# A decoder layer on one core: the bf16 identity copied earlier, and in the last FFN both outer convolution taps on VectorE through PSUM, rounding by ScalarE, three y buffers

## The chip, the cores and the metric

The kernel runs on one core of a Trainium2 chip. The metric is the device time of one execution in microseconds. Engines are named as in the profile: PE (TensorE), PEld (its weight loads), DVE (VectorE), ACT (ScalarE), POOL (GpSimd), SP (SyncE, here only a DMA queue).

## What is computed

The input is 4 sequences of 1024 tokens of width 512, in fp32. Three residual blocks follow each other, each on a layer norm of its input: self-attention with 16 heads and ALiBi bias; a local attention-free block with its own FFN ("cross FFN", 512 to 2048 to 512 with ReLU and layer norms); and a quantised FFN with a convolution in the middle ("last FFN"):

```python
h = bit_linear(x, w1)                     # x to 8-bit integers per token, w1 to -1, 0, 1
h = depthwise_conv1d(h.transpose(0, 2, 1), conv_w, conv_b)   # 3 taps along the tokens, and a bias
h = jax.nn.silu(h.transpose(0, 2, 1))
return bit_linear(h, w2)                  # h to 8-bit integers per token: scale = 127 / max|h| of the token
```

Rounding to integers is done by adding and then taking away 1.5 x 2^23 in fp32.

## The kernel before, in words

The stages run one after the other on all engines: projections, attention, `mix_in`, `mix_out`, `cross_ffn`, `quantised_ffn`. The last three share one program block: each engine has one instruction stream, written out by hand, and meets the others only through semaphores. Nothing is reordered; an instruction that waits holds all that stands behind it on its engine.

**The seam between `mix_out` and `cross_ffn`.** On POOL, `mix_out`'s `gpsimd` calls `load_vectors` (L1983, four DMA issues), then `scale_and_shift` for the last rows (two passes over each of six tiles of 128x512, and a store of each half), and then `cross_ffn`'s `gpsimd` begins, whose first instruction (L1992) copies the identity to bf16 as `ident16`. On PE, `cross_ffn`'s `tensor` begins with two waits, for `mix_out`'s last read of the PSUM banks that its own tiles lie on, and for the identity:

```python
pe.wait_ge(*before["emb"])        # DVE's last residual add, L1787
pe.wait_ge(ident16_ready, 1)
```

`ident16` itself is first used much later, to turn the quantised rows (L2056). The weights come in four chunks: SP loads (L1945, L1948), ACT rounds to the high part (L2083), DVE takes the difference (L2139).

**The last FFN.** The hidden layer is worked as 8 units (half a sequence, 512 tokens) of 16 blocks (128 hidden channels on the partitions, 512 tokens along the free axis). One slot `s` of the outer loop starts block `s`; later steps of a block stand a fixed number of slots behind (SILU_AT and so on), and every engine's stream is the same loop over slots. A block's way:

- PE multiplies it into `acc` (L2448), two banks.
- DVE multiplies by the tokens' units into `y` (`dequantise`, L2568), a row of 514 with one edge value on either side, two buffers.
- ACT copies one edge value (`set_edge`, L2523), and makes `centre` = tap 1 times y plus bias, in PSUM (L2530), and `right_tap` = tap 2 times y shifted, in SBUF (L2534).
- DVE adds tap 0 times y to `centre`, giving `conv` in SBUF (`add_left`, L2577); POOL adds `right_tap` to it (`add_right`, L2406).
- ACT applies SiLU (L2514); PE turns the block (L2457); DVE takes the maximum over its channels (`find_max`, L2585).

When 16 maxima of a unit are there, DVE works out the scales (`scales`, L2591 to L2602, five small operations and a diagonal matrix), PE spreads them over the partitions (L2465), ACT copies them out as `scale_row` (L2548). Then POOL multiplies each block by it (`scale_block`, L2412), and DVE rounds to bf16 (`round_block`, L2610), and PE makes the second product (L2475, and L2501 for the last unit). DVE adds the residual (`finish`, L2618), once in four slots. Each second unit PE also makes the products of the columns at the halves' edge (L2429), 128 small ones.

DVE's slot before is: maximum, y, left tap, rounding, and in some slots scales and `finish`. ACT's is: edge, centre, right tap, SiLU.

## Time and profile before

| | |
|---|---|
| three runs | 3474.91, 3478.45, 3482.97 us, median 3478.45 |
| profiled execution | 3476.95 us, span 3475.4 us, mean granted clock 0.967 |
| busy in the span | PE 3150.0 (91%), PEld 2284.4 (66%), DVE 2338.6 (67%), ACT 1766.6 (51%), POOL 1176.7 (34%) |
| stages by the first instruction of each | cross FFN from 2280.1 us, last FFN's slots from 3040.1 us |

The shares are an average over stages with different limits; each stage is read by itself. The profile's chain of the work that ended last covers only the last FFN here. The instructions are issued in pipeline: a timeline's next start on the same engine can lie before the listed end of the one in front.

### The profile page before, as it was taken

The numbers are of one execution on the slowest core, as the hardware profiler recorded it, in microseconds if no ns is written. First come the engines' busy times: TensorE is split into PE (matmuls) and PEld (weight loads), VectorE is DVE, ScalarE is ACT, GpSimd is POOL, SyncE is SP. The second block draws the span as 40 slices with busy tenths as digits, with TensorE's granted clock in tenths as the row PEclk, the third lists the DMA queues.
The fourth block names the chain that finished last, engine by engine and source line by source line (L and its number), as shares of the span: only waits on it lengthen the run. The fifth ranks groups of instructions, "written<-read, shape, count | busy, mean of one in ns | idle before, by whom it ended". The sixth has DMA issues, their size and how long they took to land. (4 is left out here: it accounts for less than half of the span.)

```text
span 3475.4 us, 57137 instructions
## 1 busy us (share of the span) xinstructions
PE 3150.0 (91%) x19234; PEld 2284.4 (66%) x19234; DVE 2338.6 (67%) x4193; ACT 1766.6 (51%) x3130; POOL 1176.7 (34%) x909
## 2 busy tenths in 40 slices
PE   6999899999999999979998788879999999768886
PEld 5777566666666666657776677668888888534443
DVE  5562788888888888745644588835555444589996
ACT  3331788888888888712222322232222222176662
POOL 3343411231123112244442355521111111068886
PEclk9999899999999999989999899989999999899999
DMA  6774321222122212265552644431111110300112
GB/s 215 248 238 165 98 64 58 76 77 63 58 75 76 62 57 76 76 213 210 197 202 111 183 130 123 142 111 41 41 43 42 41 43 31 110 25 31 62 49 67
DMA packets 239351, 350.53 MB, mean 101 GB/s; under 512 B 31792, under 2 KB 129104, under 8 KB 239184
## 3 DMA queue, kind: packets, MB, share of 16 engines
q1 hardware_dynamic: 208256, 290.41, 25.9%
q0 software_dynamic: 8912, 32.82, 2.9%
q10 hardware_dynamic: 22016, 25.17, 2.0%
q8 instruction: 93, 1.52, 0.2%
q14 instruction: 74, 0.61, 0.1%
HBM read 210.68 MB, written 137.64 MB: 100 GB/s over the span
## 5 line engine op out<-in xcount | busy, mean ns | idle before, releaser
L887 DVE CUSTOM_DVE_ANT_0 attend_scores<-attend_scores,attend_bias_table 128x1024 f32<-128x1024 f32 x512 | 630.4, 1231 | 164.5 <-PE attend_scores L741 161.2
L814 ACT ACTIVATE attend_probs<-attend_scores,attend_neg_max 128x1024 f32<-128x1024 f32 x512 | 571.3, 1116 | 141.1 <-DVE attend_neg_max L887 131.0
L753 PE MATMUL attend_turned<-ident,attend_probs 128*128 128x128 f32 x4096 | 557.4, 275 | 12.6 <-DVE attend_probsT L895 12.5
L753 PEld LDWEIGHTS attend_turned<-ident,attend_probs 128*128 128x128 f32 x4096 | 473.2, 141 | 120.9 <-DVE attend_probsT L895 29.8
L741 PE MATMUL attend_scores<-attend_k_stack,attend_q_stack 96*128 96x512 f32 x1024 | 373.7, 447 | 17.8 <-DMA attend_q_stack<-qk_parts 14.7
L822 ACT COPY attend_probsT<-attend_turned 128x512 f32<-128x512 f32 x640 | 359.1, 583 | 24.7 <-PE attend_turned L753 23.1
L2235 DVE TENSOR_TENSOR cross_ffn_h_lo<-cross_ffn_hidden,cross_ffn_h_hi 128x512 fp32r<-128x512 f32 x128 | 96.0, 755 | 363.9 <-ACT cross_ffn_h_hi L2126 363.2
L703 POOL TENSOR_TENSOR attend_out_parts<-attend_out_full,attend_out_parts 128x256 fp32r<-128x256 f32 x64 | 46.5, 726 | 847.1 <-ACT attend_out_parts L829 847.1
L768 PE MATMUL attend_out_acc<-attend_probsT,attend_v_in 128*32 128x256 f32 x4096 | 312.9, 390 | 0.7 <-DVE attend_out_full L905 0.7
L741 PEld LDWEIGHTS attend_scores<-attend_k_stack,attend_q_stack 96*128 96x128 f32 x1024 | 154.4, 190 | 174.7 <-issue 157.3
L895 DVE COPY attend_probsT<-attend_turned 128x512 f32<-128x512 f32 x384 | 263.5, 686 | 1.3 <-PE attend_turned L753 1.3
L2123 ACT ACTIVATE cross_ffn_hidden<-cross_ffn_h_acc,cross_ffn_b_cols 128x512 f32<-128x512 f32 x128 | 88.2, 689 | 282.3 <-PE cross_ffn_h_acc L2030 263.3
L2028 PE MATMUL cross_ffn_h_acc<-cross_ffn_aT_hi,cross_ffn_w_hi 128*128 128x512 f32 x512 | 200.4, 391 | 23.4 <-POOL cross_ffn_ident L1992 22.7
L697 POOL TENSOR_TENSOR attend_bias_table<-attend_neg_distance,attend_slope_now 128x1920 f32<-128x1920 f32 x64 | 214.8, 3387 | 1.4 <-POOL attend_slope_now L689 0.2
L2406 POOL TENSOR_TENSOR quantised_ffn_conv<-quantised_ffn_conv,quantised_ffn_right_tap 128x512 f32<-128x512 f32 x128 | 177.9, 1390 | 96.6 <-DVE quantised_ffn_conv L2577 96.5
L2041 PE MATMUL cross_ffn_out_acc<-cross_ffn_w_hi,cross_ffn_h_hi 128*128 128x512 f32 x512 | 204.2, 399 | 4.4 <-DVE cross_ffn_h_lo L2235 4.4
L2126 ACT CAST cross_ffn_h_hi<-cross_ffn_hidden 128x512 fp32r<-128x512 f32 x128 | 79.6, 622 | 239.2 <-PE cross_ffn_out_acc L2043 238.2
L2029 PE MATMUL cross_ffn_h_acc<-cross_ffn_aT_hi,cross_ffn_w_lo 128*128 128x512 f32 x512 | 200.2, 391 | 0.0
L2030 PE MATMUL cross_ffn_h_acc<-cross_ffn_aT_lo,cross_ffn_w_hi 128*128 128x512 f32 x512 | 200.0, 391 | 0.0
L2042 PE MATMUL cross_ffn_out_acc<-cross_ffn_w_lo,cross_ffn_h_hi 128*128 128x512 f32 x512 | 200.0, 391 | 0.0
L2043 PE MATMUL cross_ffn_out_acc<-cross_ffn_w_hi,cross_ffn_h_lo 128*128 128x512 f32 x512 | 199.8, 390 | 0.0
L2412 POOL TENSOR_TENSOR quantised_ffn_h_scaled<-quantised_ffn_h,quantised_ffn_scale_row 128x512 f32<-128x512 f32 x128 | 162.9, 1275 | 12.6 <-ACT quantised_ffn_scale_row L2548 7.9
(291 smaller groups left out, 6650.0 us busy)
## 6 DMA issues: line engine op xcount, KB each, us to landing
qk_parts<-qkv_qk_out SPq DMA_DIRECT2D x64, 512.0 KB, 3.2
attend_k_stack<-qk_parts SPq DMA_DIRECT2D x192, 128.0 KB, 2.5
attend_q_stack<-qk_parts SPq DMA_DIRECT2D x192, 128.0 KB, 2.7
qkv_wq_raw<-L_ffn_w POOLq DMA_DIRECT2D x16, 1024.0 KB, 7.6
o_parts<-attend_out_parts ACTq DMA_DIRECT2D x64, 256.0 KB, 2.5
carried_o_in<-o_parts SPq DMA_DIRECT2D x32, 512.0 KB, 6.2
qkv_x_in<-x SPq DMA_DIRECT2D x8, 1024.0 KB, 5.9
v_rows<-qkv_v_out SPq DMA_DIRECT2D x32, 256.0 KB, 3.4
```

Source lines behind the costliest of these rows:

```text
L697: pool.tensor_tensor(bias_table[:, h], neg_distance[:, :], slope_now[:, h:h + 1].to_broadcast([P, SPAN]), ALU.mult).then_inc(table_ready, 1)
L741: last = pe.matmul(scores[:, i % 2, k * HALF:(k + 1) * HALF], q_stack[:, h, queries], k_stack[:, h, k * HALF:(k + 1) * HALF], start=True, ...
L753: last = pe.transpose(turned[:, x, c], probs[:, i % 2, k * P:(k + 1) * P], ident[:, :])
L768: last = pe.matmul(out_acc[rows, 0:QG], v_in[:, c, rows], probsT[:, (qg - 1) % 2, c, h], start=(c == 0), stop=(c == TB - 1))
L814: act.activation(probs[:, i % 2], scores[:, i % 2], ACT.Exp, bias=neg_max[:, i % 4:i % 4 + 1], scale=-1.0, accum_out=den[:, qg % 2, j, h:h ...
L822: act.copy(probsT[:, qg % 2, x * HB:(x + 1) * HB, h, j * P:(j + 1) * P], turned[:, x]).then_inc(copied[x], 1)
L887: dve.tensor_tensor_reduce(scores[:, i % 2], scores[:, i % 2], bias_table[:, h, at:at + T], -1.0, BIG, ALU.add, ALU.min, neg_max[:, i % 4: ...
L895: dve.tensor_copy(probsT[:, qg % 2, HB:TB, h, j * P:(j + 1) * P], turned[:, 1]).then_inc(copied[1], 1)
L2028: pe.matmul(out, w1_hi[:, c, cols], aT_hi[:, c], start=c == 0, stop=False)
L2029: pe.matmul(out, w1_lo[:, c, cols], aT_hi[:, c], start=False, stop=False)
L2030: last = pe.matmul(out, w1_hi[:, c, cols], aT_lo[:, c], start=False, stop=c == KB - 1)
L2041: pe.matmul(out_acc[:, t], hi, w2_hi[:, j], start=j == 0, stop=False)
```

## The change

`load_vectors` now ends with the bf16 copy of the identity, and `gpsimd` of the cross FFN no longer begins with it. In the last FFN, `add_left` writes its sum back to `centre` in PSUM, and a new `add_right` on DVE adds the third tap from y into `conv`; POOL's `add_right` and ACT's right tap are gone. Rounding of the first seven units goes to ACT as two passes (`round_up` in place, `round_down` to bf16), with the SiLU between them; the last unit's stays on DVE (`round_last`) with a semaphore of its own. y has three buffers; the taps are added two slots behind y instead of one, and SiLU, turn, maximum, spread, scaling and rounding come one slot earlier. The waits that guard y and `centre` now name `right_added`; constants' waits count 9 memsets instead of 5.

```diff
@@ cross_ffn: load_vectors, gpsimd
                 pool.dma_start(tile[:, :], row(vector, 0, D)).then_inc(rows_loaded, 16)
+            pool.tensor_copy(ident16[:, :], ident[:, :]).then_inc(ident16_ready, 1)
 
         def gpsimd(pool):
-            pool.tensor_copy(ident16[:, :], ident[:, :]).then_inc(ident16_ready, 1)
@@ quantised_ffn: constants and tiles
+    YR = 3
-    SILU_AT, TURN_AT, MAX_AT = 3, 4, 5
-    SPREAD_AT, SCALE_AT, ROUND_AT = HB + 5, HB + 6, HB + 7
+    TAPS_AT, SILU_AT, TURN_AT, MAX_AT = 2, 2, 3, 4
+    SPREAD_AT, SCALE_AT, ROUND_AT = HB + 4, HB + 5, HB + 6
-        y = sb("y", [P, 2, 2, HALF + 2])
+        y = sb("y", [P, 2, YR, HALF + 2])
-        right_tap = sb("right_tap", [P, 2, HALF])
+        round_up_col = sb("round_up_col", [P, 1])
+        round_down_col = sb("round_down_col", [P, 1])
@@ gpsimd
+            pool.memset(round_up_col[:, :], ROUND).then_inc(const_step, 1)
+            pool.memset(round_down_col[:, :], -ROUND).then_inc(const_step, 1)
-            for s in range(2):
+            for s in range(YR):
                 pool.memset(y[:, 0, s, 0:1], 0.0).then_inc(const_step, 1)
                 pool.memset(y[:, 1, s, HALF + 1:], 0.0).then_inc(const_step, 1)
-            def add_right(i):
-                pool.wait_ge(right_ready, i + 1)
-                pool.wait_ge(left_added, i + 1)
-                pool.tensor_tensor(conv[:, i % CR], conv[:, i % CR], right_tap[:, i % 2], ALU.add).then_inc(right_added, 1)
             def scale_block(i):
                 u, f = divmod(i, HB)
                 pool.wait_ge(scale_row_ready, u + 1)
-                past(pool, hq_ready, i - 1)
+                if u == LAST and f >= 2:
+                    pool.wait_ge(last_hq_ready, f - 1)
+                else:
+                    past(pool, hq_ready, i - 1)
@@ scalar
+            def round_up(i):
+                act.wait_ge(h_scaled_ready, i + 1)
+                act.activation(h_scaled[:, i % 2], h_scaled[:, i % 2], ACT.Identity, bias=round_up_col[:, :]).then_inc(h_raised, 1)
+
+            def round_down(i):
+                u, f = divmod(i, HB)
+                act.wait_ge(h_raised, i + 1)
+                if f == 0:
+                    past(act, out_ready, (u - 1) * HT)
+                act.activation(hqT[:, u % 2, f], h_scaled[:, i % 2], ACT.Identity, bias=round_down_col[:, :]).then_inc(hq_ready, 1)
@@ scalar: taps_of
-                past(act, left_added, i - 1)
+                past(act, right_added, i - 1)
...
-                past(act, right_added, i - 1)
-                act.wait_ge(y_edged, i + 1)
-                act.activation(right_tap[:, i % 2], y[:, s, i % 2, 2:HALF + 2], ACT.Identity, scale=taps[:, f, 2:3])\
-                    .then_inc(right_ready, 1)
@@ scalar: loop over slots
                     taps_of(s)
+                r = block_at(s, ROUND_AT)
+                if r is not None and r < LAST * HB:
+                    round_up(r)
                 i = block_at(s, SILU_AT)
                 if i is not None:
                     silu(i)
+                if r is not None and r < LAST * HB:
+                    round_down(r)
@@ vector
             def add_left(i):
...
+                dve.scalar_tensor_tensor(out=centre[:, i % 2], in0=y[:, u % 2, i % YR, 0:HALF], scalar=taps[:, f, 0:1], in1=centre[:, i % 2],
+                                         op0=ALU.mult, op1=ALU.add).then_inc(left_added, 1)
+
+            def add_right(i):
+                u, f = divmod(i, HB)
+                dve.wait_ge(left_added, i + 1)
                 past(dve, silu_done, i - CR + 1)
-                dve.scalar_tensor_tensor(out=conv[:, i % CR], in0=y[:, u % 2, i % 2, 0:HALF], scalar=taps[:, f, 0:1], in1=centre[:, i % 2],
-                                         op0=ALU.mult, op1=ALU.add).then_inc(left_added, 1)
+                dve.scalar_tensor_tensor(out=conv[:, i % CR], in0=y[:, u % 2, i % YR, 2:HALF + 2], scalar=taps[:, f, 2:3], in1=centre[:, i % 2],
+                                         op0=ALU.mult, op1=ALU.add).then_inc(right_added, 1)
...
-            def round_block(i):
+            def round_last(f):
+                i = LAST * HB + f
                 dve.wait_ge(h_scaled_ready, i + 1)
...
+                dve.tensor_scalar(hqT[:, LAST % 2, f], h_scaled[:, i % 2], ROUND, -ROUND, ALU.add, ALU.add).then_inc(last_hq_ready, 1)
@@ vector: loop over slots
+                c = block_at(s, TAPS_AT)
+                if c is not None:
+                    add_left(c)
                 i = block_at(s, MAX_AT)
                 if i is not None:
                     find_max(i)
+                if c is not None:
+                    add_right(c)
                 if s < SLOTS:
                     dequantise(s)
-                i = block_at(s, 1)
-                if i is not None:
-                    add_left(i)
                 i = block_at(s, ROUND_AT)
-                if i is not None:
-                    round_block(i)
+                if i is not None and i >= LAST * HB:
+                    round_last(i - LAST * HB)
```


## Rows read from the trace of the kernel before

**Rows 1.** Busy time by stretch: stretch, length, each engine, clock, DMA share, GB/s.
```profile
2400.00:2900.00 500.00, 495.44 (x2281) 405.09 (x2280) 242.53 (x585) 136.62 (x219) 59.14 (x44) 1.00 0.13 40
3110.00:3300.00 190.00, 154.17 (x968) 79.92 (x967) 177.04 (x287) 128.01 (x253) 163.22 (x125) 0.95 0.17 54
```

**Rows 2.** Timeline, PE: start, us, line, out<-in, count, [idle before <-releaser].
```profile
2280.10 0.77 PE L2028 MATMUL cross_ffn_h_acc<-cross_ffn_aT_hi,cross_ffn_w_hi 128*128 128x512 f32 x1 [22.69 <-POOL cross_ffn_ident L1992]
```

**Rows 3.** Timeline, POOL, around the cross FFN's start.
```profile
2249.37 1.31 POOL L1574 TENSOR_TENSOR mix_out_z<-mix_out_z,mix_out_gamma_row 128x512 f32<-128x512 f32 x1
...
2279.70 0.30 POOL L1992 CAST cross_ffn_ident<-ident 128x128 bf16<-128x128 f32 x1
```

**Rows 4.** Timeline, DVE, a slot of the last FFN with an output.
```profile
3321.08 0.73 DVE L2577 SCALAR_TENSOR_TENSOR quantised_ffn_conv<-quantised_ffn_y,quantised_ffn_taps,quantised_ffn_centre 128x512 f32<-128x512 f32 x1
3321.73 0.87 DVE L2610 TENSOR_SCALAR quantised_ffn_hqT<-quantised_ffn_h_scaled 128x512 bf16<-128x512 f32 x1
3322.53 0.74 DVE L2618 SCALAR_TENSOR_TENSOR quantised_ffn_out<-quantised_ffn_out_acc,quantised_ffn_h_unit,quantised_ffn_x_in 128x512 f32<-128x512 f32 x1
3323.19 0.67 DVE L2585 TENSOR_REDUCE quantised_ffn_block_max<-quantised_ffn_turned 128x4 f32<-128x512 f32 x1
3323.79 0.68 DVE L2568 TENSOR_TENSOR quantised_ffn_y<-quantised_ffn_acc,quantised_ffn_unit_row 128x512 f32<-128x512 f32 x1
```

**Rows 5.** Timeline, DVE, a short rounding.
```profile
3314.24 0.41 DVE L2610 TENSOR_SCALAR quantised_ffn_hqT<-quantised_ffn_h_scaled 128x512 bf16<-128x512 f32 x1
```

**Rows 6.** Timeline, POOL, in the slot of rows 4.
```profile
3321.05 1.27 POOL L2412 TENSOR_TENSOR quantised_ffn_h_scaled<-quantised_ffn_h,quantised_ffn_scale_row 128x512 f32<-128x512 f32 x1
```

**Rows 7.** Timeline, DVE, the end of the stage before the cross FFN.
```profile
2262.14 0.68 DVE L1787 TENSOR_TENSOR mix_out_z<-mix_out_acc,mix_out_emb_in 128x512 f32<-128x512 f32 x1
...
2266.88 3.81 DVE L1798 TENSOR_SCALAR mix_out_z<-mix_out_z,mix_out_moments,mix_out_rstd 128x512 f32<-128x512 f32 x4
```

**Rows 8.** Timeline, ACT, its first read of the cross FFN.
```profile
2284.94 0.69 ACT L2123 ACTIVATE cross_ffn_hidden<-cross_ffn_h_acc,cross_ffn_b_cols 128x512 f32<-128x512 f32 x1 [26.76 <-PE cross_ffn_h_acc L2030]
```

**Rows 9.** Timeline, SP queue, and DMA issues with median us to landing.
```profile
2262.25 0.37 SPq L1948 DMA_DIRECT2D cross_ffn_x_in<-L_xattn_w  x1
...
cross_ffn_x_in<-L_xattn_w SPq DMA_DIRECT2D x4, 1024.0 KB, 6.8
```

**Rows 10.** Groups by line: busy us, mean ns, idle before.
```profile
L2188 DVE SCALAR_TENSOR_TENSOR cross_ffn_z<-cross_ffn_z,cross_ffn_rstd,cross_ffn_x_in 128x512 f32<-128x512 f32 x32 | 21.9, 745 | 0.0
```

**Rows 11.** Timeline, ACT, early in the last FFN.
```profile
3048.88 0.17 ACT L2523 COPY quantised_ffn_y<-quantised_ffn_edges 128x1 f32<-128x1 f32 x1
3048.96 0.78 ACT L2530 ACTIVATE quantised_ffn_centre<-quantised_ffn_y,quantised_ffn_conv_bias,quantised_ffn_taps 128x512 f32<-128x512 f32 x1
3049.68 0.71 ACT L2534 ACTIVATE quantised_ffn_right_tap<-quantised_ffn_y,quantised_ffn_taps 128x512 f32<-128x512 f32 x1
3050.29 0.61 ACT L2514 ACTIVATE quantised_ffn_h<-quantised_ffn_conv 128x512 f32<-128x512 f32 x1
```

**Rows 12.** Timeline, DVE, y of slots 5, 21, 25 and 127.
```profile
3052.08 0.69 DVE L2568 TENSOR_TENSOR quantised_ffn_y<-quantised_ffn_acc,quantised_ffn_unit_row 128x512 f32<-128x512 f32 x1 [1.21 <-PE quantised_ffn_acc L2448]
...
3089.95 0.68 DVE L2568 TENSOR_TENSOR quantised_ffn_y<-quantised_ffn_acc,quantised_ffn_unit_row 128x512 f32<-128x512 f32 x1
...
3103.83 0.69 DVE L2568 TENSOR_TENSOR quantised_ffn_y<-quantised_ffn_acc,quantised_ffn_unit_row 128x512 f32<-128x512 f32 x1 [3.40 <-PE quantised_ffn_acc L2448]
...
3410.53 0.67 DVE L2568 TENSOR_TENSOR quantised_ffn_y<-quantised_ffn_acc,quantised_ffn_unit_row 128x512 f32<-128x512 f32 x1
```

**Rows 13.** Timeline, DVE, scale arithmetic: first, next maximum, the y that waits.
```profile
3330.67 0.21 DVE L2591 TENSOR_REDUCE quantised_ffn_h_max<-quantised_ffn_block_max 128x4 f32<-128x64 f32 x1
...
3333.97 0.69 DVE L2585 TENSOR_REDUCE quantised_ffn_block_max<-quantised_ffn_turned 128x4 f32<-128x512 f32 x1
...
3339.07 0.69 DVE L2568 TENSOR_TENSOR quantised_ffn_y<-quantised_ffn_acc,quantised_ffn_unit_row 128x512 f32<-128x512 f32 x1 [1.57 <-PE quantised_ffn_acc L2448]
```

**Rows 14.** Timeline, ACT, the last scale row.
```profile
3426.64 0.58 ACT L2548 COPY quantised_ffn_scale_row<-quantised_ffn_spread 128x512 f32<-128x512 f32 x1 [9.56 <-PE quantised_ffn_spread L2465]
```

More of the change, by code:

```diff
@@ L2519, in set_edge @@
                 act.wait_ge(edges_done, u // 2 + 1)
-                past(act, left_added, i - 1)
-                past(act, right_ready, i - 1)
+                past(act, right_added, i - YR + 1)
                 edge = slice(HALF + 1, HALF + 2) if s == 0 else slice(0, 1)
-                act.copy(y[:, s, i % 2, edge], edges[:, u // 2 % 2, f, 1 - s:2 - s]).then_inc(y_edged, 1)
+                act.copy(y[:, s, i % YR, edge], edges[:, u // 2 % 2, f, 1 - s:2 - s]).then_inc(y_edged, 1)
             def taps_of(i):
@@ L2528, in taps_of @@
                 act.wait_ge(y_ready, i + 1)
[L2529 to L2530 removed]
+                past(act, right_added, i - 1)
+                act.activation(centre[:, i % 2], y[:, s, i % YR, 1:HALF + 1], ACT.Identity, bias=conv_bias[:, f:f + 1],
                                scale=taps[:, f, 1:2]).then_inc(centre_ready, 1)
[L2532 to L2535 removed]
             for s in range(END):
@@ L2626, in vector @@
                     find_max(i)
+                if c is not None:
+                    add_right(c)
                 if s < SLOTS:
                     dequantise(s)
-                i = block_at(s, 1)
-                if i is not None:
-                    add_left(i)
                 i = block_at(s, ROUND_AT)
-                if i is not None:
-                    round_block(i)
+                if i is not None and i >= LAST * HB:
+                    round_last(i - LAST * HB)
                 u = half_at(s, HB + MAX_AT - 1)
```

27 lines of the change are left out of this document (11 added, 16 removed).

## The prediction

> **What bounds the kernel now.** I read the busy table first (PE 91%, no other engine above 67%), then the 40 slices, and saw that the two edits fall into stretches with different bounds, so I asked for busy time by stretch. From 2400 to 2900 us (cross FFN) the PE is busy 495.44 of 500 us: whatever lets this stretch begin earlier moves everything behind it. From 3110 to 3300 us (last FFN) the PE has 154 of 190 us, DVE 177 and POOL 163: DVE sets the pace there, with POOL just under it [rows 1].
>
> The list of waits has one entry made by a single instruction: the first product of the cross FFN (L2028) sat 22.69 us and was released by GpSimd's bf16 copy of the identity, 2279.70 to 2280.00 [rows 2, 3]. The timeline of each engine around it shows that this copy stood behind eight scalings that had nothing to do with it.
>
> In the last FFN the timeline of one slot (one 128x512 block) is what to read. DVE instructions start one after the other some 0.08 us before the former's listed end, so I count start to start: left tap 0.65, rounding 0.80, output 0.66, maximum 0.60, and y 0.60 (0.68 less 0.08) [rows 4]. The rounding is odd: listed at 0.87 there and 0.41 elsewhere [rows 4, 5]. In the long form it ends 0.3 us behind the end of the GpSimd scaling that was running (3321.05 + 1.27 = 3322.32, against 3322.60) [rows 4, 6]: it waits for GpSimd's instruction to end, then takes its 0.33. So a slot without an output is 0.60 + 0.60 + 0.65 + 0.80 = 2.65 us; where an output falls in, the next rounding is short, and four slots with one output take 10.80, or 2.70 a slot.
>
> **Part 1, the identity.** The copy goes to the end of the vector loads, just ahead of the scaling that starts at 2249.37 [rows 3], so it is there at 2249.7. What is late next? The PE's other wait there is for DVE's last read of the old PSUM banks: 2262.14 + 0.68 = 2262.82 [rows 7]; the first weight splits stand ahead of that on DVE's queue, so they are done. The PE starts at 2262.9 instead of 2280.1: **-17.2 us**.
>
> Does it hold it? ScalarE reads the first block 4.84 us after the PE starts [rows 2, 8], now at 2267.7. DVE is busy with its normalising until 2266.88 + 3.81 = 2270.7 [rows 7], so the first low part comes some 1.5 us later than ScalarE would allow, but the PE has three blocks of 12 products of its own before it needs it. The second weight chunk was issued at 2262.25 and needs 6.8 us [rows 9]: 2269.1, and ScalarE comes to it at about 2270.8. GpSimd's 0.30 us at 2249 is covered, since its next scalings wait for the normalising that starts at 2266.88 [rows 7]. If a cover fails it costs 1 to 2 us. I keep -17.2, with -15 and -18 as ends.
>
> **Part 2, the last FFN.** DVE gives up the rounding in seven of eight units (0.33 to 0.80 a slot) and takes the right tap, of the same kind as the left one: 0.65. Its slot becomes left 0.66, maximum 0.60, right 0.66, y 0.60 = **2.52 us**, and nothing in it is of the kind that waited for GpSimd.
>
> The left tap now writes PSUM. No row shows DVE do that. The nearest rows: the left tap with one PSUM input 0.73, the output with one 0.74, the same operation all in SBUF 0.745 [rows 4, 10]. So a PSUM side has cost nothing; DVE's 512-column passes of all kinds lie within 0.07 us, and I bound the write by that on both sides, at 0.00. 128 times 0.07 is 9 us either way.
>
> The Trainium skill ("VectorE: DVE Perf Modes", the section on the TRN2 errata) gives a Vector pass 120 fixed cycles from PSUM against 58 in SBUF, at 0.96 GHz. By it an access through PSUM would cost 0.065 us more, a left tap of 0.80 us; this trace does not agree for reads (0.73 against 0.745), and of the write it shows nothing.
>
> ScalarE: its starts, unhindered, are edge 0.08, centre 0.72, right tap 0.61, SiLU 0.52 [rows 11]. It drops the right tap and adds two roundings, each with one pointer operand like the right tap: 0.08 + 0.72 + 0.61 + 0.52 + 0.61 = 2.54 us. That is DVE's 2.52, and under its 2.52 + 0.66/4 = 2.69 with outputs. The second rounding waits for the first, but the SiLU stands between. ScalarE's SiLU ends 2.67 us after the start of the y two slots ahead; with 0.7 for the turn the maximum can have it at 3.45 and asks at 3.78. The margin is 0.3 us.
>
> GpSimd is left with one 1.27 us pass a slot: off the path. Three y buffers and the new lags take waits of neighbours away; five more small memsets run in GpSimd's idle time ahead of the stage.
>
> The sum, by stretches, in the time of the profiled run [rows 12]:
> (a) Before any rounding exists DVE has only maximum, y and left tap, 1.85, and a slot takes about 2.2; now 2.52. The pipeline fills through the same turn and product, so the sixth y (3052.08) comes perhaps 0.6 later; then 16 slots x 2.52 + 1.6 of scale arithmetic = 41.9, where 3089.95 - 3052.08 = 37.9 stood. **+4.6**.
> (b) From y 21 (3089.95) to y 127 (3410.53): 320.6 us for 106 slots. Now 106 x 2.52 = 267.1; 22 outputs x 0.66 = 14.5; six times the scale arithmetic. That took 3.30 (3330.67 to 3333.97) [rows 13]; five small operations at the 0.21 of the first and a diagonal matrix of 0.6 would be 1.6, so half of it goes in waits for GpSimd, in the manner of the rounding. With GpSimd half idle I take one such wait of two: 2.6 x 6 = 15.6 (ends 1.6 and 3.3). Behind it y waited 1.57 for the PE [rows 13]; the maximum now comes 0.66 later in the slot but y 1.6 later: 0.7 is left, and 0.3 on the next turn; six of these, 5.9. The three edge products stopped y for 3.4 [rows 12]; by the same count 2.9 once and 2.3 twice, 0.6 behind each: 9.4. Sum 312.5: **-8.1**.
> (c) The end. From y 127 to the last scale row (3426.64) are 16.1 us [rows 12, 14], a queue of roundings on DVE, each waiting for GpSimd. Now DVE is free, and ScalarE's queue sets it, counted from y 127: y 0.7, centre 0.7, two slots of rounding, SiLU, rounding (1.74 each) and one more rounding 0.6 bring the last SiLU to its start at 5.5; SiLU, turn and maximum 2.1 more, 7.6; scales 2.6 and spread 1.3, 11.5, by when ScalarE has done its other roundings (10.8). **-4.6**. The last unit's rounding stays on DVE in the old form, so the 48 us behind it stay.
>
> Part 2: 4.6 - 8.1 - 4.6 = -8.1. With part 1: -25.3. The profiled execution took 3476.95 us (span 3475.4); it gives 3451.7. The median of the runs is 1.5 above it; I round between the two: **3452 us**.
>
> **Rivals.**
> *More is won* (3443 us). The scale arithmetic meets no GpSimd instruction (6 x 1.0) and the PE stalls behind it vanish (some 4 us). For it: GpSimd is idle half of each slot. Against: its scaling is released by ScalarE's rounding, whose end falls at the start of the arithmetic.
> *The left tap is dearer through PSUM* (3461 us): the upper bound above, 0.07 x 128 = 9 us, all on DVE's path. Part 2 is then worth nothing. For it: a write is not a read. Against: no row has a PSUM side cost anything. The Trainium skill's rule named above is this case too.
> *The identity was not the last* (3469 us): something else holds the PE, or the cross FFN gives the time back, and part 2 alone is left. Against: a PE at 99% behind it [rows 1] has no room to give back.
> *ScalarE becomes the bound* (3482 us, slower). If its passes do not overlap once two are rounding in place with waits, a slot costs full durations: 0.17 + 0.78 + 0.71 + 0.61 + 0.71 = 2.98 [rows 11], 0.29 more than 2.69; over the 106 slots +30: 3451.7 + 30. It makes the kernel slower from 2.93 us a slot, and reduces the gain from 2.7. For it: the margin is 0.02 to 0.15 us. Against: ScalarE's starts overlap in rows 11 although neighbours wait for DVE.
>
> **Chances.** Forecast 0.50, more is won 0.22, dearer left tap 0.18, identity 0.05, ScalarE 0.05. The range 3440 to 3468 holds the first three with their own ends and leaves out the last two and some of the edges. A measurement here tells 0.2% (7 us) from no change: below 3471.5 lie all but the ScalarE rival and a corner of the identity rival: faster 0.93, same 0.03, slower 0.04.
>
> **What will show it.** Part 1: the first product of the cross FFN at 2262.9, released by DVE's L1787, and the last FFN's first y 17 us earlier than 3040.13. Part 2: left and right taps at 0.73; no rounding on DVE before the last unit; y every 2.52 us in plain slots, and 2.2 nowhere; ScalarE nearly without idle time; the scale arithmetic near 2.6 with one long member; 11 to 12 us from the last y to the scale row. I am wrong if a slot reads 2.6 or more (then see whether the left tap or a wait for ScalarE is longer), or if the PE's first product waits for another releaser after 2262.9.

## The result and the profile after

| | before | after |
|---|---|---|
| runs on one chip, median | 3478.78 us (3474.91 to 3482.97, 4 runs) | 3451.53 us (3447.61 to 3454.87, 4 runs) |
| profiled execution, span | 3476.95, 3475.4 us | 3454.87, 3453.2 us |
| DVE, ACT, POOL busy in the span | 2338.6, 1766.6, 1176.7 us | 2349.5, 1818.8, 1009.2 us |

The ratio is 0.9921, with a 95% interval of 0.9904 to 0.9938: 27.5 us less (21.6 to 33.4). The forecast was 3452.

The two profiled executions differ by 22.2 us and not by 27, because the work ahead of the seam took 6.3 us longer in the one of after: DVE's last L1787 starts at 2268.44 there and at 2262.14 before [rows 7]. So each stretch below is counted from its own first instruction.

Busy time by stretch, after (columns as in [rows 1]). The cross FFN is as full as before. In the last FFN ACT went from 128 to 169 us of 190 and POOL from 163 to 82: the work went to ACT.

```profile
2400.00:2900.00 500.00, 496.14 (x2285) 405.90 (x2284) 235.94 (x572) 136.59 (x220) 53.89 (x40) 1.00 0.13 39
3110.00:3300.00 190.00, 162.79 (x1022) 83.47 (x1020) 182.80 (x301) 169.37 (x330) 82.47 (x66) 0.97 0.18 59
```

The seam, PE's timeline: the first product, and the one wait in the 18 us behind it. The first answers to [rows 2]: 5.49 us idle, released by DVE's L1787, where GpSimd's copy had released it after 22.69.

```profile
2269.18 0.80 PE L2028 MATMUL cross_ffn_h_acc<-cross_ffn_aT_hi,cross_ffn_w_hi 128*128 128x512 f32 x1 [5.49 <-DVE mix_out_z L1787]
...
2287.09 0.50 PE L2041 MATMUL cross_ffn_out_acc<-cross_ffn_w_hi,cross_ffn_h_hi 128*128 128x512 f32 x1 [2.46 <-DVE cross_ffn_h_lo L2235]
```

The second is new. From the first product to the last FFN's first y it was 760.03 us before (3040.13 less 2280.10, [rows 2]), now 762.39 (3031.57 less 2269.18): 2.4 us of the 17.2 were given back. DVE's timeline behind the normalising, after, shows by whom:

```profile
2276.97 1.78 DVE L2235 TENSOR_TENSOR cross_ffn_h_lo<-cross_ffn_hidden,cross_ffn_h_hi 128x512 fp32r<-128x512 f32 x1
2278.68 3.38 DVE L2139 TENSOR_TENSOR cross_ffn_w_lo<-cross_ffn_z,cross_ffn_w_hi 128x2048 fp32r<-128x2048 f32 x1
2281.99 3.38 DVE L2139 TENSOR_TENSOR cross_ffn_w_lo<-cross_ffn_x_in,cross_ffn_w_hi 128x2048 fp32r<-128x2048 f32 x1
2285.29 3.44 DVE L2235 TENSOR_TENSOR cross_ffn_h_lo<-cross_ffn_hidden,cross_ffn_h_hi 128x512 fp32r<-128x512 f32 x2
2290.85 6.68 DVE L2235 TENSOR_TENSOR cross_ffn_h_lo<-cross_ffn_hidden,cross_ffn_h_hi 128x512 fp32r<-128x512 f32 x2 [2.12 <-ACT cross_ffn_h_hi L2126]
2298.10 2.29 DVE L2139 TENSOR_TENSOR cross_ffn_w_lo<-cross_ffn_z,cross_ffn_w_hi 128x2048 fp32r<-128x2048 f32 x1 [0.57 <-ACT cross_ffn_w_hi L2083]
```

And POOL's in the same microseconds:

```profile
2278.29 1.62 POOL L1576 TENSOR_TENSOR mix_out_z<-mix_out_z,mix_out_beta_row 128x512 f32<-128x512 f32 x1
2279.88 3.34 POOL L1574 TENSOR_TENSOR mix_out_z<-mix_out_z,mix_out_gamma_row 128x512 f32<-128x512 f32 x1
2283.30 3.19 POOL L1576 TENSOR_TENSOR mix_out_z<-mix_out_z,mix_out_beta_row 128x512 f32<-128x512 f32 x1
...
2291.33 5.04 POOL L1998 TENSOR_TENSOR cross_ffn_a_in<-cross_ffn_a_in,cross_ffn_b_row 128x512 f32<-128x512 f32 x4
```

Read the two together. L2139 starts at 2278.68 while POOL's pass runs to 2279.91; it ends at 2282.06, which is 2.15 behind that, about its free 2.29. POOL's next pass starts at 2279.88 and ends at 2283.22, 1.16 behind DVE's. Here they take turns, a whole instruction each. It does not always go one for one: of the two L2235 from 2290.85 the first is listed with 6.08 us (free: 0.69) and ends 0.56 behind the last of four GpSimd passes. The Trainium skill ("SBUF — State Buffer", section "Who interferes with whom") says that a DVE instruction with two SBUF inputs contends with a GpSimd one that reads SBUF, and that the lock is exclusive; the trace agrees (3.38 for 2.29). Before, the PE's late start had put GpSimd's passes ahead of DVE's splits.

The last FFN, DVE's timeline, a slot with an output after the scale arithmetic (answers to [rows 4]): y to y 3.17, of which 0.66 is the output, so 2.51 for a plain slot.

```profile
3223.84 0.68 DVE L2577 TENSOR_TENSOR quantised_ffn_y<-quantised_ffn_acc,quantised_ffn_unit_row 128x512 f32<-128x512 f32 x1
3224.44 0.74 DVE L2633 SCALAR_TENSOR_TENSOR quantised_ffn_out<-quantised_ffn_out_acc,quantised_ffn_h_unit,quantised_ffn_x_in 128x512 f32<-128x512 f32 x1
3225.10 0.74 DVE L2585 SCALAR_TENSOR_TENSOR quantised_ffn_centre<-quantised_ffn_y,quantised_ffn_taps,quantised_ffn_centre 128x512 f32<-128x512 f32 x1
3225.75 0.68 DVE L2600 TENSOR_REDUCE quantised_ffn_block_max<-quantised_ffn_turned 128x4 f32<-128x512 f32 x1
3226.35 0.73 DVE L2592 SCALAR_TENSOR_TENSOR quantised_ffn_conv<-quantised_ffn_y,quantised_ffn_taps,quantised_ffn_centre 128x512 f32<-128x512 f32 x1
3227.01 0.68 DVE L2577 TENSOR_TENSOR quantised_ffn_y<-quantised_ffn_acc,quantised_ffn_unit_row 128x512 f32<-128x512 f32 x1
```

By line over the whole stage the left tap (L2585, into PSUM) takes 743 ns, the right tap (L2592) 734. ACT's timeline, a slot: 0.08 + 0.72 + 0.61 + 0.52 + 0.61 = 2.54, one start right behind the other.

```profile
3252.14 0.17 ACT L2532 COPY quantised_ffn_y<-quantised_ffn_edges 128x1 f32<-128x1 f32 x1
3252.22 0.78 ACT L2539 ACTIVATE quantised_ffn_centre<-quantised_ffn_y,quantised_ffn_conv_bias,quantised_ffn_taps 128x512 f32<-128x512 f32 x1
3252.94 0.71 ACT L2517 ACTIVATE quantised_ffn_h_scaled<-quantised_ffn_h_scaled,antised_ffn_round_up_col 128x512 f32<-128x512 f32 x1
3253.55 0.61 ACT L2513 ACTIVATE quantised_ffn_h<-quantised_ffn_conv 128x512 f32<-128x512 f32 x1
3254.07 0.71 ACT L2524 ACTIVATE quantised_ffn_hqT<-quantised_ffn_h_scaled,tised_ffn_round_down_col 128x512 bf16<-128x512 f32 x1
```

The four points of [rows 12 and 14], after: y 5, 21 and 127 (DVE), and the last scale row (ACT).

```profile
3043.30 0.68 DVE L2577 TENSOR_TENSOR quantised_ffn_y<-quantised_ffn_acc,quantised_ffn_unit_row 128x512 f32<-128x512 f32 x1
...
3085.08 0.68 DVE L2577 TENSOR_TENSOR quantised_ffn_y<-quantised_ffn_acc,quantised_ffn_unit_row 128x512 f32<-128x512 f32 x1
...
3392.73 0.68 DVE L2577 TENSOR_TENSOR quantised_ffn_y<-quantised_ffn_acc,quantised_ffn_unit_row 128x512 f32<-128x512 f32 x1
```

```profile
3404.49 0.58 ACT L2558 COPY quantised_ffn_scale_row<-quantised_ffn_spread 128x512 f32<-128x512 f32 x1 [0.65 <-PE quantised_ffn_spread L2464]
```

| stretch | before | after | difference | forecast |
|---|---|---|---|---|
| PE's wait at the seam | 22.69 | 5.49 | -17.2 | -17.2 |
| first product to first y | 760.03 | 762.39 | +2.4 | 0 |
| (a) y 0 to y 21 | 49.82 | 53.51 | +3.7 | +4.6 |
| (b) y 21 to y 127 | 320.58 | 307.65 | -12.9 | -8.1 |
| (c) y 127 to the scale row | 16.11 | 11.76 | -4.4 | -4.6 |
| scale row to the end | 48.76 | 48.71 | 0 | 0 |

The sum is -28.4 (forecast -25.3); with the 6.3 us ahead of the seam it is the 22.2 between the spans.

What is left over in (b) is at the scale arithmetic. PE's timeline there, before: 3.60 us idle, then the turn, the spread and the product, all slow. The granted clock from 3139 to 3143 is 0.50, the lower of its two levels (1.2 GHz); from 3125 to 3134 it was 1.00.

```profile
3134.07 1.03 PE L2475 MATMUL quantised_ffn_out_acc<-quantised_ffn_w2T,quantised_ffn_hqT 128*128 128x512 bf16 x4
3138.70 1.09 PE L2457 MATMUL quantised_ffn_turned<-ident,quantised_ffn_h 128*128 128x128 f32 x4 [3.60 <-DVE quantised_ffn_block_max L2585]
3139.57 1.92 PE L2465 MATMUL quantised_ffn_spread<-quantised_ffn_diag,quantised_ffn_ones 128*128 128x512 f32 x2
3141.28 1.92 PE L2448 MATMUL quantised_ffn_acc<-quantised_ffn_xqT,quantised_ffn_w1T 128*128 128x512 bf16 x4
```

One of before's places shows what the clock alone does: behind the same 3.60 us of idle time it stayed at 1.00 (3186 to 3190), the product took 1.03, and DVE did not wait.

```profile
3186.87 0.63 PE L2457 MATMUL quantised_ffn_turned<-ident,quantised_ffn_h 128*128 128x128 f32 x4 [3.60 <-DVE quantised_ffn_block_max L2585]
...
3188.19 1.03 PE L2448 MATMUL quantised_ffn_acc<-quantised_ffn_xqT,quantised_ffn_w1T 128*128 128x512 bf16 x4
```

After, the PE is idle for 1.95 us at such a place (there is one to each unit). At three of the six between y 21 and y 127 everything that follows is in the short form, at a granted clock of 1.00:

```profile
3362.69 0.63 PE L2456 MATMUL quantised_ffn_turned<-ident,quantised_ffn_h 128*128 128x128 f32 x4 [1.95 <-DVE quantised_ffn_block_max L2600]
3363.15 1.02 PE L2464 MATMUL quantised_ffn_spread<-quantised_ffn_diag,quantised_ffn_ones 128*128 128x512 f32 x2
3364.01 1.03 PE L2447 MATMUL quantised_ffn_acc<-quantised_ffn_xqT,quantised_ffn_w1T 128*128 128x512 bf16 x4
```

At the other three (spreads at 3129.21, 3223.88 and 3317.41) the clock fell to 0.50 all the same:

```profile
3224.74 1.86 PE L2447 MATMUL quantised_ffn_acc<-quantised_ffn_xqT,quantised_ffn_w1T 128*128 128x512 bf16 x4
```

DVE's waits for the PE behind the arithmetic (over 0.25 us) add up to 0.88 + 3.04 + 1.36 + 1.51 + 1.57 + 1.58 = 9.9 us before, and to 1.23 + 0.44 + 0.57 = 2.2 after. All but the first of before's six (0.88) stand where the clock had fallen, and so do all three of after's.

### The profile page after: what moved, and what is told of

It reads as the page before. It is cut to its first block and busy times, and to the rows that moved or that the text cites. A ratio compares the mean times of both kernels' runs of the same rounds, so it can differ in the third digit from the quotient of the medians.

```text
span 3453.2 us, 56869 instructions
## 1 busy us (share of the span) xinstructions
PE 3149.6 (91%) x19234; PEld 2281.7 (66%) x19234; DVE 2349.5 (68%) x4209; ACT 1818.8 (53%) x3226; POOL 1009.2 (29%) x785
## 5 line engine op out<-in xcount | busy, mean ns | idle before, releaser
L753 PE MATMUL attend_turned<-ident,attend_probs 128*128 128x128 f32 x4096 | 556.5, 275 | 12.6 <-DVE attend_probsT L895 12.5
L2235 DVE TENSOR_TENSOR cross_ffn_h_lo<-cross_ffn_hidden,cross_ffn_h_hi 128x512 fp32r<-128x512 f32 x128 | 104.3, 820 | 340.0 <-ACT cross_ffn_h_hi L2126 339.4
L294 POOL TENSOR_TENSOR qkv_qk_out<-qkv_qk_full,qkv_qk_out 128x512 fp32r<-128x512 f32 x64 | 94.4, 1480 | 182.6 <-ACT qkv_qk_out L420 182.3
```

The lines of the kernel that those rows point to most:

```text
L753: last = pe.transpose(turned[:, x, c], probs[:, i % 2, k * P:(k + 1) * P], ident[:, :])
```

## The experiments

Gains over before are the ratio times 3479 us; two kernels are compared by their ratios, since not all ran on one chip. An interval is 3 to 6 us to either side, so the stretches of the profiles decide where the runs can't.

### e1_identity: the first edit alone

```diff
             for tile, vector in ((b2_row, b2), (gamma_row, gamma), (beta_row, beta)):
                 pool.dma_start(tile[:, :], row(vector, 0, D)).then_inc(rows_loaded, 16)
+            pool.tensor_copy(ident16[:, :], ident[:, :]).then_inc(ident16_ready, 1)
 
         def gpsimd(pool):
-            pool.tensor_copy(ident16[:, :], ident[:, :]).then_inc(ident16_ready, 1)
```

> The kernel before with the first edit alone (GpSimd's copy of the identity moved ahead of its last scalings). Theory A (the identity alone held the PE; GpSimd's eight last passes and VectorE's splits, kept apart before, now meet and slow each other): the PE's wait ahead of the cross FFN's first product falls from 22.7 to about 5.5 us (-17.2), the stretch from that product to the last FFN's first y grows by 2.4 (760.0 to 762.4), and the median falls by 14.8 us, to about 3464. Rival B (the 2.4 us belong to the second edit or to that one execution): the stretch stays at 760.0 and the gain is 17.2. Rival C (part 1 is worth more, and part 2 less, than predicted): over 18 us here.

Median 3465.50, ratio 0.9954 (0.9940 to 0.9968): -16.0. PE's wait is 5.49, and first product to first y is 3028.62 - 2266.47 = 762.15: theory A, -17.2 + 2.1 at the seam. Its last FFN, the same code as before, took 439.6 us from first y to end, where before's took 435.3: behind the scale arithmetic there were 17.5 us of waits in seven places instead of 9.9 in six, and the clock fell at all seven. That term of the old kernel differs by some microseconds from one execution to the next.

### e2_ffn: the second edit alone

The kernel after, with the two changed lines of the diff above put back.

> The kernel after with the identity's copy put back behind the scalings, that is, the second edit alone. Theory A (the two edits add up, and the last FFN gives 13.7 and not 8.1): the wait ahead of the cross FFN is 22.7 again, first product to first y 760.0, first y to the end 421.6, and the median is about 3465 (-13.5). Rival B (part 2 is worth the predicted 8.1, the rest was the execution's own): 427.2 in that stretch and about 3470.5.

Median 3463.77, ratio 0.9952 (0.9938 to 0.9965): -16.7. PE's wait is 22.71, first product to first y 759.92, first y to end 421.0. Theory A; B's 427.2 is out. So the second edit is worth 14.3 against before's own execution, 18.6 against e1's, and the forecast of 8.1 is low either way. The two medians give 16.0 + 16.7 where both edits together gave 27.5; each is known to 5 us, and the stretches do add up: 15.1 at the seam and 14.3 in the last FFN, 29.4 against 28.4.

### e3_short_scalings and e7_seam_dve: GpSimd's last passes taken away

e3 leaves most of them out, e7 gives their work to VectorE.

```diff
-            scale_and_shift(B - 1, 1, range(HT))
+            scale_and_shift(B - 1, 1, range(HT), cols=8)      # e3: z[:, h, t, 0:cols]
```
```diff
+                    if isinstance(b, int) and b == B - 1 and h == 1:                  # e7
+                        for j in range(HT):
+                            dve.scalar_tensor_tensor(out=z[:, h, j], in0=z[:, h, j], scalar=moments[:, j, 0:1], in1=gamma_row[:, :],
+                                                     op0=ALU.subtract, op1=ALU.mult).then_inc(norm_ready, 1)
...
+                            dve.scalar_tensor_tensor(out=z[:, h, j], in0=z[:, h, j], scalar=rstd[:, j:j + 1], in1=beta_row[:, :],
+                                                     op0=ALU.mult, op1=ALU.add).then_inc(last_shifted, 1)
```

> The kernel after, but GpSimd's eight gamma and beta passes on the last half batch of the stage before the cross FFN act on 8 of its 512 columns, so most of that half is left unscaled. Theory A (these passes and VectorE's operations with two SBUF inputs slow each other, which costs the cross FFN 2.4 us): VectorE's low parts of h (L2235) take 0.69 and its z additions (L2139) 2.3 from the first on, no 2.46 us wait of the PE for a low part stands in the first 15 us, first product to first y is 760.0, and the median falls by some 2.4 us, to 3449. Rival B (VectorE is late there for its own queue: the normalising that ends at 2270.7 and the splits behind it): L2235 still 1.8 to 6, the stretch still 762.4, no change of time. Rival C (a transfer of the second chunk's weights is late): the PE's wait stays, and names a DMA or SyncE's queue behind VectorE.

> The kernel after, but the last half batch ahead of the cross FFN has its mean, gamma, deviation and beta applied by VectorE in eight passes (each with two SBUF inputs, 0.745 us alone) in place of four passes of VectorE (3.88 us together) and eight of GpSimd. Same result. Theory A (GpSimd's eight passes beside VectorE's splits make the 2.4 us loss): with them gone L2235 and L2139 are back at 0.69 and 2.3 us, VectorE begins them some 1.5 us later, the PE's wait of 2.46 shrinks to below 1, and the kernel gains 1 to 2.5 us, 3449 to 3450. Rival B (what counts is only when VectorE gets to its first low part, and eight passes are later than four): no gain or a loss of 1 to 2 us.

e3: median 3446.73, ratio 0.9908, -4.5 against after. e7: 3449.58, ratio 0.9915, -2.1. Neither has the PE's wait of 2.46. First product to first y is 759.46 and 759.52. The runs by themselves could not show 2.4 us; this stretch can:

| GpSimd's eight passes | kernels | first product to first y |
|---|---|---|
| beside the splits | after, e1, e4, e5, e6, e10, e11 | 762.06 to 762.62 |
| ahead of them (old seam) | before, e2, e9 | 759.85 to 760.03 |
| not there | e3, e7, e12 | 759.46 to 759.97 |

DVE's timeline in e7: the low part and the splits at their free durations, although they begin 9.3 us behind the PE's first product (2268.12), 1.5 later than in after. From 2278.92 on it was GpSimd that waited: its next pass was listed with 5.95 us (the row below has two passes) until DVE's four were through, and nothing hung on it.

```profile
2277.43 0.68 DVE L2247 TENSOR_TENSOR cross_ffn_h_lo<-cross_ffn_hidden,cross_ffn_h_hi 128x512 fp32r<-128x512 f32 x1
2278.03 2.28 DVE L2151 TENSOR_TENSOR cross_ffn_w_lo<-cross_ffn_z,cross_ffn_w_hi 128x2048 fp32r<-128x2048 f32 x1
2280.24 2.28 DVE L2151 TENSOR_TENSOR cross_ffn_w_lo<-cross_ffn_x_in,cross_ffn_w_hi 128x2048 fp32r<-128x2048 f32 x1
```
```profile
2278.92 7.19 POOL L2010 TENSOR_TENSOR cross_ffn_a_in<-cross_ffn_a_in,cross_ffn_b_row 128x512 f32<-128x512 f32 x2
```

One part of e3's theory A did not hold: its second L2139 still took 3.39 and the two L2235 behind it 3.48, since GpSimd now went on sooner to L1998 and met them there. That cost nothing, for no product of the PE waited for them.

### e4_left_sbuf: the left tap into SBUF

```diff
-                dve.scalar_tensor_tensor(out=centre[:, i % 2], ..., in1=centre[:, i % 2],
+                dve.scalar_tensor_tensor(out=left[:, i % 2], ..., in1=centre[:, i % 2],
...
-                dve.scalar_tensor_tensor(out=conv[:, i % CR], ..., in1=centre[:, i % 2],
+                dve.scalar_tensor_tensor(out=conv[:, i % CR], ..., in1=left[:, i % 2],
```

> The kernel after, but the left tap writes an SBUF tile and the right tap reads it from there, so the right tap has two SBUF inputs. Theory A (a PSUM side costs next to nothing by itself, and what PSUM buys is that no VectorE pass with two SBUF inputs meets GpSimd's scaling): the left tap stays at 0.73 to 0.75, the right tap is 0.75 in stretches in which GpSimd doesn't scale (the first 60 us of the stage) and 1.0 to 1.5 where it does; a plain slot grows from 2.51 to 2.9 or more, and the kernel loses 25 to 50 us. Rival B (only passes in a two-port mode wait for GpSimd, two plain inputs don't): the slot stays at 2.51 and the time within 2 us. Rival C (a PSUM access costs 0.06 us more each): left and right taps come down to 0.67, the slot to 2.4, and the kernel gains 10 us.

Median 3458.51, ratio 0.9934 (0.9921 to 0.9948): 4.5 us slower than after, and y 0 to y 127 took 368.90 where after took 361.16. The sign is theory A's, the size is not. By line and shape over 3040 to 3400 us, right tap and left tap of e4:

```profile
L2593 DVE SCALAR_TENSOR_TENSOR quantised_ffn_conv<-quantised_ffn_y,quantised_ffn_taps,quantised_ffn_left 128x512 f32<-128x512 f32 x123 | 96.4, 783 | 0.0
L2586 DVE SCALAR_TENSOR_TENSOR quantised_ffn_left<-quantised_ffn_y,quantised_ffn_taps,quantised_ffn_centre 128x512 f32<-128x512 f32 x122 | 89.7, 736 | 0.0
```

The left tap came down from 743 to 736 ns: a PSUM write costs 7 ns a pass, 0.9 us in all. The right tap with two SBUF inputs went from 734 to 783 on average: 0.73 or 0.74 in 62 of 128, 0.75 to 0.78 in 35, 0.84 to 0.87 in 28, where it starts some 0.3 us before the end of GpSimd's one pass in a slot, and over 1 us in three. The two meet only by their edges, so the lock costs 0.05 us a slot and not the 0.4 I had expected; the scale arithmetic took 2.67 where after has 2.48.

### e11_two_y: two y buffers

```diff
-    YR = 3
+    YR = 2
```

> The kernel after with two y buffers in place of three (the right tap of a block then has to be done before its buffer's next y). Theory A (the third buffer only uncouples neighbours; VectorE's own order has the right tap of the block two back ahead of y anyway, but ScalarE's edge copy and y's second read now meet): the slot stays at 2.51 and the time within 3 us of after. Rival B (ScalarE, which is almost without idle time, has to wait for the right tap before it may write the edge, is then late with the centre tap, and the left tap with it): the slot grows to 2.7 to 3.0 and the kernel loses 20 to 50 us, all of what the second edit won. Rival C (the stalls behind the scale arithmetic come back, since y can't run ahead): +1 to 2 us at each of six places, +8.

Median 3471.83, ratio 0.9981 (0.9972 to 0.9990): 20.9 us slower than after, most of what the second edit had won. That is rival B's size, but not its place. DVE's timeline in e11:

```profile
3104.67 0.74 DVE L2592 SCALAR_TENSOR_TENSOR quantised_ffn_conv<-quantised_ffn_y,quantised_ffn_taps,quantised_ffn_centre 128x512 f32<-128x512 f32 x1
3105.50 0.69 DVE L2577 TENSOR_TENSOR quantised_ffn_y<-quantised_ffn_acc,quantised_ffn_unit_row 128x512 f32<-128x512 f32 x1
3106.11 0.75 DVE L2585 SCALAR_TENSOR_TENSOR quantised_ffn_centre<-quantised_ffn_y,quantised_ffn_taps,quantised_ffn_centre 128x512 f32<-128x512 f32 x1
3106.76 0.69 DVE L2600 TENSOR_REDUCE quantised_ffn_block_max<-quantised_ffn_turned 128x4 f32<-128x512 f32 x1
```

Right tap to y is 0.83 where it is 0.66 in after. With two buffers y has to wait for the end of the right tap, which is the instruction just ahead of it on the same engine, so the two can no longer overlap. The slot is 2.69, and 0.17 x 128 is 22 us. ScalarE is not what holds the slot: over 3100 to 3400 it waits 32.6 us (20.0 for y, 12.6 for the right tap), and 31.8 in after. Rival C did not show: behind the arithmetic y waited 0.85 us at the first place and 0.29 at one other.

### e9_warm_before: the kernel before, with the PE kept busy

```diff
+                for again in range(4 if half_at(i, SPREAD_AT) is not None else 1):
+                    for c in range(KB):
+                        last = pe.matmul(acc[:, i % ACC], w1T[:, c, f * P:(f + 1) * P], ...
```

> The kernel before with one thing added: in the slot in which VectorE does a unit's scale arithmetic, TensorE does that slot's block product four times over (same operands, same result), so that it works through most of the 3.60 us that it sat idle there. Theory A (the six waits of y behind the arithmetic, 0.88, 2.69 + 0.35, 1.36, 1.51, 1.57 and 1.58 = 9.9 us before against 2.2 after, come of the granted clock, which had fallen in that idle time: the spread took 1.92 and the product 1.92 where 1.03 is usual): with the idle time filled, turned comes down from 1.09 to 0.63 and the product from 1.92 to 1.03, the waits vanish, and the kernel gains 8 to 10 us over before with none of the change in it. Rival B (the waits come of the order of the work, turn, spread and product all behind one maximum, and the third y buffer and the shorter lags of the change took them away): the waits stay at 1 us or more each and the time within 2 us of before. Rival C (the added products make the turn late): slower by up to 6 x 1 us.

Median 3471.56, ratio 0.9982 (0.9972 to 0.9991): -6.3, with none of the change in it. PE's timeline at one of the places:

```profile
3132.76 3.62 PE L2449 MATMUL quantised_ffn_acc<-quantised_ffn_xqT,quantised_ffn_w1T 128*128 128x512 bf16 x16
3136.21 1.03 PE L2476 MATMUL quantised_ffn_out_acc<-quantised_ffn_w2T,quantised_ffn_hqT 128*128 128x512 bf16 x4
3138.24 0.63 PE L2458 MATMUL quantised_ffn_turned<-ident,quantised_ffn_h 128*128 128x128 f32 x4 [1.01 <-DVE quantised_ffn_block_max L2586]
3138.71 1.02 PE L2466 MATMUL quantised_ffn_spread<-quantised_ffn_diag,quantised_ffn_ones 128*128 128x512 f32 x2
```

Twelve products that nobody needs bring the turn from 1.09 to 0.63 and the spread from 1.92 to 1.02. The waits behind the arithmetic fell from 9.9 us to 1.3 (0.48 + 0.28 + 0.54). Theory A, with less gain than its 8 to 10: the added products made y 21 come 0.6 later, and the waits at the edge products stayed (10.4 before, 10.3 here). So it was the clock that had made before's waits. That the change took most of them away by shortening the PE's idle time is read from counts, not from a run of its own. Of the six places of each profile between y 21 and y 127, the clock was at 0.50 within 4 us of the spread's start at:

| PE's idle time ahead of the turn | profiles | places |
|---|---|---|
| 3.6 us | before, e1 | 11 of 12 |
| 2.3 us | e4, e11 | 5 of 12 |
| 1.8 to 2.2 us | after, e2, e3, e5, e6, e7, e10, e12 | 15 of 48 |
| 1.0 us | e9 | 0 of 6 |

### e10_edges, e5_early_finish, e6_ramp: three things the profile of after pointed to

```diff
-                if s % (2 * HB) == HB + 8 and s // (2 * HB) + 1 < B:                  # e10, PE
-                    edge_products(pe, s // (2 * HB) + 1)
+                k = s % (2 * HB) - HB - 7
+                if 0 <= k < 8 and s // (2 * HB) + 1 < B:
+                    edge_products(pe, s // (2 * HB) + 1, range(2 * k, 2 * k + 2))
```
```diff
+                    if s == TAIL + (0, 2, 4, 7)[j]:                                   # e5, DVE
+                        finish((LAST - 1) * HT + j)
```
```diff
+                if i < RAMP:                                # e6: left tap to SBUF, right tap on ACT, add on POOL
+                    past(dve, silu_done, i - CR + 1)
+                    out = conv[:, i % CR]
```

In e10 VectorE also reads the edges later, in slot HB + 15 instead of HB + 9. Of e6 only the core is shown.

> The kernel after, but the 128 one-column edge products, which stand in one piece of 3.46 us behind one slot (three times in the stage), are spread over eight slots, 16 in each. Theory A (behind the piece y waits for TensorE: 3.52, 2.05 + 0.94 and 1.97 = 8.5 us, made up of the piece itself and of products at half clock behind it; a slot has 0.4 us of TensorE's time to spare, as much as a share takes): the waits vanish but for some tenths, gain 6 to 8 us over after, the median near 3444. Rival B (a share in each of eight slots is too much beside the products, turned is late by 0.2 to 0.4 us a slot): the gain is 2 or less. Rival C (small products let the clock fall for all the eight slots): slower than after by several us.

> The kernel after, with the four outputs of the last unit but one placed earlier among VectorE's last roundings (one every two or three blocks in place of one every four). Theory A (TensorE sat 8.26 us ahead of its last products, for the third of these outputs, though its product had long been done): the last products begin about 8 us sooner behind the last scale row, the stretch from the last scale row to the end falls from 48.7 to about 41, and the median to about 3444. Rival B (the last products wait for the last rounding, which VectorE and GpSimd make at 2.97 us for two blocks): the end stays, gain 0 to 1. Rival C (the early outputs wait for TensorE's product and hold up the roundings): slower by 1 to 3 us.

> The kernel after, but for the first 18 blocks of the last FFN, before any rounding exists, the right tap is done as before (ScalarE multiplies it into SBUF, GpSimd adds it). Theory A (the second edit costs 3.7 us there, since VectorE's fourth pass of 0.66 makes the slot 2.51 where it was 2.22, and ScalarE and GpSimd stand half idle): the slot falls to 2.22 or below (ScalarE's four starts add up to 1.93, VectorE's three passes to 1.86), y 0 to y 21 takes 44 to 50 us in place of 53.5, and the kernel gains 4 to 9 us over after, some 3444. Rival B (the slot goes back to 2.22 by the PE's turn and product, but the switch to the new form empties the pipeline once): gain 1 to 3. Rival C (the hand-over between three engines is late): no gain.

e10: median 3443.47, ratio 0.9901 (0.9887 to 0.9916), 7.0 faster than after. Of the 8.5 us of waits at the edge products none over 0.25 is left; a share of 16 takes the PE 0.41 us in a slot that had more than that to spare, and the clock stayed at 1.00 through all three sets of shares, so rival C is out. y 21 to y 127 took 296.9 where after took 307.7: the 8.5, and some 2 us because the clock fell at one place behind the arithmetic and not at three. e5: 3443.53, ratio 0.9900 (0.9885 to 0.9915), 7.3 faster; scale row to end 42.8 where it was 48.7. The last products began 17.64 us behind the scale row, not 23.89, and still waited 4.22 for an output: theory A, with 5.9 of its 8 us, since the last output can't come before the roundings ahead of it on VectorE (2.97 us for two blocks). PE's timeline in after and in e5:

```profile
3428.38 1.01 PE L2500 MATMUL quantised_ffn_out_acc<-quantised_ffn_w2T,quantised_ffn_hqT 128*128 128x512 bf16 x2 [8.26 <-DVE quantised_ffn_out L2633]
```
```profile
3414.36 1.01 PE L2501 MATMUL quantised_ffn_out_acc<-quantised_ffn_w2T,quantised_ffn_hqT 128*128 128x512 bf16 x2 [4.22 <-DVE quantised_ffn_out L2634]
```

e6: 3442.04, ratio 0.9890 (0.9875 to 0.9905), 10.8 faster, of which the stretch shows 7.6; y 0 to y 21 takes 45.92 us (3028.37 to 3074.29) where after takes 53.51, below before's 49.82. The slot there is 1.94 (DVE's timeline in e6), close to ScalarE's 1.93; before, the same work took 2.22 (y 5 to y 20, 33.3 us), with two y buffers and longer lags; which of the two made the 0.28 was not tried.

```profile
3047.83 0.69 DVE L2611 TENSOR_TENSOR quantised_ffn_y<-quantised_ffn_acc,quantised_ffn_unit_row 128x512 f32<-128x512 f32 x1
...
3049.77 0.69 DVE L2611 TENSOR_TENSOR quantised_ffn_y<-quantised_ffn_acc,quantised_ffn_unit_row 128x512 f32<-128x512 f32 x1
```

### e12_all: the version that beats both

After with the edits of e5, e6, e7 and e10.

> The kernel after with four changes at once: the edge products in eight shares, the last outputs placed earlier, the old right tap in the first 18 blocks, and the seam's last scaling on VectorE. If they add up (edge products 8, outputs 6 to 8, first blocks 4 to 8, seam 0 to 2.4) the kernel gains 18 to 26 us over after and stands at 3426 to 3434. If the first blocks or the seam bring nothing: 3436 to 3438.

Median 3424.13 us (3418.89 to 3428.78, 5 runs), ratio 0.9840 (0.9826 to 0.9854): 55.7 us under before, 28.2 under after. The four alone gave 7.3, 10.8, 2.1 and 7.0, together 27.2: they add up. So do the stretches of the profiles (2.9 at the seam, 7.6, 10.8 and 6.0 alone, 27.3; 27.5 in e12), which leave out what differs between executions elsewhere. First y to end is 396.65 us, where after has 421.6 and before 435.3.

## Why the prediction came out

**Part 1, -17.2: right, and its cover not.** The releaser, DVE's L1787, and the 17.2 us are as forecast. I went through the covers (ScalarE, DVE, the weights' transfer, GpSimd) as queues, and put DVE's lateness at 1.5 us with no cost. What failed is the step that counted DVE's and GpSimd's passes at the durations they had when they stood apart. Brought together they hold each other up, L2235 takes 1.74 to 1.78, once 6.08, and L2139 3.38, and 2.4 us come back (e3, e7). The lateness itself was harmless, as forecast: in e7 the low part came later still and no product waited. I had read the same effect in the rounding [rows 4, 6] without asking where else it would now appear.

**(a) +4.6: right (+3.7).** The first five slots lost nothing, where I had put 0.6.

**(b) -8.1: mis-sized, -12.9.** By its terms:
- Slot 2.52: measured 2.51. (The margin of the maximum was added up wrongly, 2.67 + 0.7 is 3.37 and not 3.45, and the new memsets are four and not five; nothing hung on either.) The left tap through PSUM costs 7 ns more (e4); the rival that gave it 70 falls.
- Outputs 0.66 each, and 9.4 lost at the edge products: measured 0.66, and 9.2 by the excess of those slots over 2.51.
- Scale arithmetic 2.6: measured 2.48 (3219.45 to 3221.92), with one member waiting for GpSimd, L2612 with 1.09, as forecast.
- Stalls behind it, 5.9: measured 2.5 by the same count (1.31, 0.53 and 0.66 at three places, nothing at three). This is the term that failed; with it 106 x 2.51 + 22 x 0.66 + 6 x 2.48 + 9.2 + 2.5 = 307.2, where 307.65 stood. I took before's wait of 1.57 [rows 13] as a matter of order (turn, spread and product behind one maximum) and subtracted the slots' shift from it. So the forecast has a stall of 1.0 at each of six places. In (b) a stall appears only where the PE's clock had fallen to half; e9 shows on the kernel before that without the fall it is gone. With 1.95 us of idle time instead of 3.60 the clock fell at three places of six, not at five. At those three the order counts as I had it: 0.5 to 1.3 is left of before's 1.4 to 3.0. At the others the wait is gone.

**(c) -4.6: right (-4.4)**, and the tail behind the scale row did not move.

**The third y buffer** I had waved through in half a sentence. It is what makes the slot of 2.51 possible (e11): 0.17 us a slot, 21 us.

**Rivals.** "More is won" gave 3443, from no port wait in the arithmetic (wrong) and vanished stalls (3.4 of the 5.9). "The identity was not the last" did not come, but what I put against it (a PE at 99% has no room to give back) did not hold: 2.4 us came back. "ScalarE becomes the bound" did not come: its starts overlap as in [rows 11] with both roundings in place. That the forecast met the median within 1 us is partly luck: 2.4 us too much at the seam and 5.5 too little in the last FFN leave 3 too little, inside the interval of the runs.

**Open.** What the 6.3 us ahead of the seam are: over the ten profiled executions with the new seam the first product starts between 2261.6 and 2269.5 us, as wide a spread as the runs of one kernel show in their times. No run took that apart. Why the clock fell behind 1.95 us of idle time at three places of after and not at the other three, and behind 3.60 at all but one of twelve, is not settled either: it falls at other places in other executions, and the size of this term is partly chance.

## What to carry to other kernels

When a wait goes, list which instructions will now run at the same time on VectorE and GpSimd, and price those with two SBUF inputs anew: their old durations were measured apart. A matmul engine's stall behind a gap should first be read for its clock (is the same product 1.9 us where it is 1.0 elsewhere?), for then the length of the gap matters and not only the order of the work: filling the gap removed the stall (e9), and a shorter gap made it rarer (from 5 of 6 places to 3 of 6). And an instruction that waits for the one just ahead of it on its own engine loses their overlap, 0.17 us here; one more buffer gives it back.

## What the runs showed of the hardware

- VectorE, 128x512 fp32, (scalar op) op: 734 ns with one SBUF and one PSUM input and an SBUF output, 743 with a PSUM output, 745 with two SBUF inputs in the cross FFN [rows 10], and 0.73 to 0.74 us so in e4 where no GpSimd pass ran.
- VectorE passes with two SBUF inputs and GpSimd's passes hold each other up. Where they alternate, 2.29 becomes 3.38 and 1.26 becomes 3.34 and 3.19. Not always one for one: a VectorE pass of 0.69 took 6.08 beside four of GpSimd's (after), and a GpSimd pass of some 1.3 took 5.95 beside VectorE's, which kept their 2.28 and 0.68 (e7).
- 128 products of one column take the PE 3.37 to 3.46 us in one piece. During the first piece of after the clock fell to 0.50, and the product behind it took 1.87 where 1.03 is usual; behind the second it fell a product later, and behind the third it stayed at 1.00. In shares of 16 they took 0.41 each (start to start) between full products at 1.02.
- Behind idle time of the PE the clock falls at some places and not at others of the same length: at 11 of 12 behind 3.6 us, 15 of 48 behind 1.8 to 2.2, none of 6 behind 1.0.
